# Softmax probabilities turned in two row halves of the matmul array

## The reference

```python
qkv = einsum('bte,fe->btf', layernorm(x), Wqkv)        # 8 heads of 64; q, k, v
q, k = q + pe, k + pe                                   # position table added
scores = einsum('bhtd,bhsd->bhts', q, k) / sqrt(64)     # causal mask
probs = softmax(scores, axis=-1)
attn = einsum('bhts,bhsd->bhtd', probs, v)
x = x + layernorm(attn_joined @ Wo.T)
x = x + layernorm(tanh(layernorm(x) @ W1 @ W2 @ W3 + bias))
```

## Time and profile before

| | |
|---|---|
| median of 3 runs | 561.28 us |
| the profiled execution | 561.25 us, span 559.4 us |
| PE busy | 537.3 us, 96% |
| PEld busy | 455.6 us, 81% |
| DVE busy | 469.5 us, 84% |
| ACT busy | 409.4 us, 73% |
| POOL busy | 398.9 us, 71% |

### The profile page before, as it was taken

The page is one execution under the profiler, slowest core; times in us unless marked ns, Lnnn a source line. Parts: engine busy times, 40 slices in busy tenths (PEclk is TensorE's granted clock), DMA queues, the critical chain, the costliest instruction groups (busy, mean ns, idle before and its releaser), DMA issues.

```text
span 559.4 us, 16795 instructions
## 1 busy us (share of the span) xinstructions
PE 537.3 (96%) x4595; PEld 455.6 (81%) x4595; DVE 469.5 (84%) x2063; ACT 409.4 (73%) x1507; POOL 398.9 (71%) x650
## 2 busy tenths in 40 slices
PE   7799999999999999999999999999999999999971
PEld 4588888888888888888888888888888888888850
DVE  4987898888889888888888888988888888888843
ACT  2777877778778777777877877777787787777740
POOL 3535777877777787777787777778777777776653
PEclk9999999999999999999999999999999999999985
DMA  5000011100000100000100010011000011100000
GB/s 160 29 2 21 11 30 30 30 19 28 20 18 28 28 28 19 28 17 21 28 28 25 22 28 9 28 28 28 19 28 24 14 28 28 28 9 21 21 9 19
DMA packets 27963, 14.53 MB, mean 26 GB/s; under 512 B 1700, under 2 KB 27431, under 8 KB 27943
## 3 DMA queue, kind: packets, MB, share of 16 engines
q1 hardware_dynamic: 27510, 13.51, 8.5%
q10 hardware_dynamic: 432, 0.79, 0.4%
HBM read 10.09 MB, written 4.19 MB: 26 GB/s over the span
## 4 chain that ended last, share of the span: by engine, by line
PE 92%; DVE 3%; ACT 2%; issue 1%; DMA 1%; POOL 1%; POOLq 0%; DVEq 0%; ACTq 0%
PE scores L879 18%; PE turned_and_heads L933 17%; PE misc_bank L994 11%; PE qk_bank L894 6%; PE qk_bank L896 5%; PE qk_bank L895 5%; PE turned_probs L910 5%; PE turned_probs L911 5%; PE turned_and_heads L919 5%; PE misc_bank L865 4%; PE misc_bank L977 3%; PE misc_bank L867 3%; PE misc_bank L866 3%; PE misc_bank L939 2%; PE misc_bank L975 1%
## 5 line engine op out<-in xcount | busy, mean ns | idle before, releaser
L263 ACT ACTIVATE probs<-scores,neg_max 128x256 f32<-128x256 f32 (+1 forms) x512 | 208.6, 425 | 43.4 <-DVE neg_max L631 43.3
L631 DVE CUSTOM_DVE_ANT_0 scores<-scores,mask 128x256 f32<-128x256 f32 (+1 forms) x512 | 166.2, 386 | 11.4 <-PE scores L879 11.4
L641 DVE TENSOR_TENSOR qk<-qk_bank,pe 128x512 f32<-128x512 f32 x128 | 87.4, 683 | 32.9 <-PE qk_bank L896 25.1
L421 POOL TENSOR_TENSOR probs<-probs,inv_sum 128x512 f32<-128x512 f32 x126 | 101.3, 823 | 12.6 <-DVE inv_sum L647 12.6
L879 PE MATMUL scores<-qk 64*128 64x256 f32 (+1 forms) x1024 | 106.6, 342 | 1.6 <-DVE qk L641 1.0
L263 ACT ACTIVATION_READ_ACCUMULATOR probs<-scores,neg_max 128x1 f32 x512 | 107.5, 210 | 0.0
L879 PEld LDWEIGHTS scores<-qk 64*128 64x128 f32 x1024 | 87.9, 186 | 18.7 <-issue 11.2
L933 PE MATMUL turned_and_heads<-pt,vals 128*64 128x256 f32 (+1 forms) x1024 | 98.5, 335 | 1.4 <-ACT pt L283 1.4
L933 PEld LDWEIGHTS turned_and_heads<-pt,vals 128*64 128x64 f32 x1024 | 64.6, 137 | 27.7 <-issue 2.0
L894 PE MATMUL qk_bank<-xt_hi,w_hi 128*128 128x256 f32 x256 | 80.5, 314 | 2.0 <-DVE qk L641 1.2
L281 ACT COPY pt<-turned_probs 128x512 f32<-128x512 f32 x128 | 76.4, 597 | 7.3 <-PE turned_probs L911 3.7
(11 more groups left out here) (91 smaller groups left out, 1013.8 us busy)
## 6 DMA issues: line engine op xcount, KB each, us to landing
x_in<-in_x SPq DMA_DIRECT2D x32, 128.0 KB, 2.2
x_res<-in_x SPq DMA_DIRECT2D x32, 128.0 KB, 2.1
out_x<-x SPq DMA_DIRECT2D x32, 128.0 KB, 1.8
w_raw<-in_w_qkv_t ACTq DMA_DIRECT2D x3, 256.0 KB, 3.8
pe<-pe_table SPq DMA_DIRECT2D x1, 256.0 KB, 5.2
wo<-in_w_o_t SPq DMA_DIRECT2D x1, 256.0 KB, 3.8
mask<-causal_mask SPq DMA_DIRECT2D x1, 128.0 KB, 5.3
w_sb<-in_w SPq DMA_DIRECT2D x2, 64.0 KB, 3.3
```

The costliest lines, as they stand in the source:

```text
L263: ins = nc.scalar.activation(probs[k][j][:, h, lo:hi], s_bank[j][:, h, lo:hi], ACT.Exp, bias=neg_max[k][j][:, i:i + 1], scale=-1.0, accum_ ...
L421: ins = nc.gpsimd.tensor_tensor(some, some, inv, ALU.mult)
L631: ins = nc.vector.tensor_tensor_reduce(some, some, mask[:, t * P:2 * P], -1.0, HIGHEST, ALU.add, ALU.min, neg_max[k][j][:, i:i + 1])
L641: nc.vector.tensor_tensor(qk[j][:, :], qk_bank[:, :], pe[:, :], ALU.add).then_inc(qk_kept, 1)
```

## The change

Each block of 128 x 128 is now turned as two blocks of 64 x 128 (rows 0 to 63 and rows 64 to 127), with a 64 x 64 piece of the identity as the moving operand. The two halves lie in the two row halves of the array and write into two different PSUM banks, so a turn is 12 instructions. The six blocks of a pair take columns 0 to 383 of both banks. `heads_bank` is now the second of these two banks. ACT's two copies each read from both banks and put the halves side by side. One semaphore, `turned`, replaces `turned0` and `turned1`. All of PE's waits for a turn stand ahead of its first instruction, followed by an increment of a semaphore that nobody waits for (`turn_begun`). turn_y stands ahead of turn (k=1, j=1) in place of behind it.

```diff
-        turn_bank = ps("turned_probs", [P, 2, T])
-        heads_bank = ps("turned_and_heads", [P, 512])
+        turned_banks = ps("turned_and_heads", [P, 2, 512])
+        heads_bank = turned_banks[:, 1, :]
...
                 wait(act, heads_made, units(b, k))
-                act.wait_ge(turned0, pairs(b, k, j + 1))
-                nc.scalar.copy(pt0[j][:, :, :], turn_bank[:, :, :]).then_inc(pt0_kept, 1)
-                act.wait_ge(turned1, pairs(b, k, j + 1))
-                nc.scalar.copy(pt1[j][:, :, :], heads_bank[:, 0:2 * P].rearrange("p (h t) -> p h t", h=2)
-                               ).then_inc(pt1_kept, 1)
+                act.wait_ge(turned, pairs(b, k, j + 1))
+                nc.scalar.copy(pt0[j][:, :, :].rearrange("p h (n f c) -> p (h n) f c", n=2, f=2),
+                               turned_banks[:, :, 0:T].rearrange("p f (n c) -> p n f c", c=D)).then_inc(pt0_kept, 1)
+                nc.scalar.copy(pt1[j][:, :, :].rearrange("p h (f c) -> p h f c", f=2),
+                               turned_banks[:, :, T:T + P].rearrange("p f (n c) -> p n f c", c=D)).then_inc(pt1_kept, 1)
...
                 wait(pe_eng, pt0_kept, pairs(b, k, j))
-                for h in range(2):
-                    nc.tensor.transpose(turn_bank[:, h, P:T], some[:, h, 0:P], ident[:, :])
-                    ins = nc.tensor.transpose(turn_bank[:, h, 0:P], some[:, h, T:SC], ident[:, :])
-                ins.then_inc(turned0, 1)
+                wait(pe_eng, pt1_kept, pairs(b, k, j))
                 if j == 0:
-
                     wait(pe_eng, heads_kept[(k + 1) % 2], b.times(1, k))
-                else:
-                    pe_eng.wait_ge(pt1_kept, pairs(b, k, 1))
-                for h in range(2):
-                    ins = nc.tensor.transpose(heads_bank[:, h * P:(h + 1) * P], some[:, h, P:T], ident[:, :])
-                ins.then_inc(turned1, 1)
+
+                pe_eng.sem_inc(turn_begun)
+
+                blocks = [(h, lo) for h in range(2) for lo in (T, 0)] + [(h, P) for h in range(2)]
+                for n, (h, lo) in enumerate(blocks):
+                    for f in range(2):
+                        r = slice(f * D, (f + 1) * D)
+                        ins = nc.tensor.transpose(turned_banks[:, f, n * D:(n + 1) * D], some[r, h, lo:lo + P], ident[r, r])
+                ins.then_inc(turned, 1)
...
                     turn_x(b.plus(1))
+                    turn_y(b.plus(-2))
                     turn_probs(b.plus(-1), 1, 1)
-                    turn_y(b.plus(-2))
                     make_scores(b, 1)
```

More of the change, by code:

```diff
@@ L145, in build_block @@
         scaled = [sem(f"scaled{j}") for j in range(2)]
-        turned0, turned1, pt0_kept, pt1_kept = sem("turned0"), sem("turned1"), sem("pt0_kept"), sem("pt1_kept")
+        turned, pt0_kept, pt1_kept = sem("turned"), sem("pt0_kept"), sem("pt1_kept")
+        turn_begun = sem("turn_begun")
         heads_made, heads_kept = sem("heads_made"), [sem(f"heads_kept{k}") for k in range(2)]
@@ L256, in exps @@
                     return
-                wait(act, turned1, pairs(b, k, j - 3))
+                wait(act, turned, pairs(b, k, j - 3))
                 act.wait_ge(max_found, pairs(b, k, j + 1))
```

## The result

The changed kernel takes 558.31 us (median of 14 runs, 557.06 to 560.59) against 561.13 us for the kernel before on the same chip (14 runs, 560.46 to 562.21): a ratio of 0.9952, 95% interval 0.994 to 0.9964. It is faster, by 2.8 us. The forecast was 9.3 us. Its profiled execution took 557.18 us with a span of 555.3 us, 4.1 us less than the span before. It is one of the five quickest of the 14 (557.06 to 557.23 us), so the two traces show more of a gain than the medians do.

What follows compares the result with a forecast made beforehand. PE, busy 96% of the span, was taken as the bound. One turn with its scores saves 0.30 us a batch, the others zero: 561.25 - 31 x 0.30 (9.3) = 552.0 us, range 545 to 564.

Steps and rivals of the forecast that it cites:

- The distance between pairs: In each new turn, pairs of half-row transposes start 0.06 us apart, with bounds 0.055 and 0.11 us.
- The change of shape: Between full-array and row-half work on PE: 0.09 us for emptying, plus up to 0.10 for an unhidden weight load.
- The lone turn (1, 0): Turn (k=1, j=0), changing shape twice: make_qk +0.03 us at most; ACT's copy late by 0.02 to 0.07 us.
- No gain behind the turn (1, 1): Scores after turn (k=1, j=1): PE could gain 0.28 us but waits that long for the DVE and ACT loop.
- No gain behind the turn (0, 0): After turn (k=0, j=0): the next weight load waits for ACT's copy of attn until 285.69, so zero gain.
- DVE in time at the scores behind the turn (0, 1): At these scores DVE is ready at 288.71, the scores come at 288.78, so DVE just lets the gain through.
- The term 31 x 0.30: Turn (k=0, j=1) with its scores saves 0.30 us per batch, 31 times between batches: 9.3 us.
- the end of the kernel: Behind the loop, ACT gets its first table after six pairs instead of four transposes: 0.3 us either way.
- the waits that moved: Earlier `heads_kept` and `pt1_kept` waits ahead of all twelve transposes: free, late bookkeeping taken at zero, bounds 0 and 0.12 us.
- Copies dearer, or the sequencer late: Rival, chance 0.13: +0.16 to +0.28 us a batch on the binding loop, 557 to 561 us.
- Both pairs gain: Rival, chance 0.12: more slack in the DVE and ACT loop lets 0.28 us come too, 18 us, 543 us.
- The distance does not shrink: Rival, chance 0.19: pairs stay 0.11 us apart, turns only add changes of shape, +0.37 x 32 = 11.8, 573 us.

Runs made afterwards that it cites:

- the cut in before: Kernel before with two 128-column ScalarE exponentials left out of each loop batch (output wrong there): period 16.30 us against 16.46; 556.39 us, one run.
- the filled pair: Kernels before and after, each with matmuls on zeros in PE's idle gaps behind the loop: 559.97 and 555.11 us, tails 42.10 and 43.20 us.
- the unfilled tails: Last batch's value projections to the end, profiled kernels without matmuls on zeros: full turns 42.35 to 43.42 us, halves 44.86 to 46.57.
- the two kernels with the cut: Kernels before and after, each with two 128-column ScalarE exponentials left out of each loop batch: periods 16.30 and 15.80 us, 0.50 apart.

## Why the prediction was wrong

**What held.** The distance between pairs: 0.06 us, as taken from the second weight load in the earlier trace rows, and so the bound on the whole change was read rightly. The change of shape, 0.09 us on either side. The lone turn (1, 0) at +0.03 us on PE. No gain behind the turn (1, 1), with PE waiting for ACT instead. The copies at their old price. No gain behind the turn (0, 0). DVE in time at the scores behind the turn (0, 1): its wait for them fell from 11.4 to 0.9 us in all. The Trainium skill states in "TensorEngine Tiling (Array Packing)", section Key Properties, that a change of the tiling mode drains the array; the 0.09 us ahead of the first pair of halves (283.54 + 0.12 to 283.75) agrees.

**The term 31 x 0.30 was mis-sized by 2.1 us.** It measured 29 x 0.25 = 7.2 us at the last batch's value projections. The turn with its scores saved 0.28, by the kernel that has it alone: the score load behind the last pair cost 0.07 us (284.11 to 284.18) in place of the 0.11 taken, but the second score pair came 0.27 us behind the first (284.18 to 284.45). It had been 0.32 before (287.96 to 288.28), and the prediction had struck off 0.10, down to 0.22. Another 0.02 is the lone turns, whose lateness at ACT (0.02 to 0.07) the prediction had worked out, found to be within ACT's slack, and left out of the sum: with the turn (0, 1) alone the period is 16.17, with all four 16.20, with the two lone ones 0.04 above before's. And the offset between the two kernels grows only from batch 3 on: at batch 2 they stand at 39.03 and 39.00 us. PE does not set the time there alone: it was busy for 14.36 of the 17.70 us from 4.3 to 22.0 in after. The prediction also took PE for the bound of the kernel before; by the cut in before, a chain through ACT was longer by 0.16 us, and the gain came in only because the turn (0, 1) lies on that chain too.

**The step that failed is the end of the kernel**, "0.3 us either way". It measured +3.04 us in the profiled runs, and 4.0 us by the medians where that form was put into before's tail, 3.5 where it was taken out of after's. The step looked at one effect only, that ACT gets its first table after six pairs in place of four transposes. It did not carry over its own paragraph on the waits that moved. That paragraph found `heads_kept` free because DVE's copy ends 0.73 us before it is needed, in the loop; it said that without this cover the cost would be the lateness itself. In the tail, nothing stands between make_heads and the next turn, the cover is gone, and the lateness is about 0.9 us at one turn. The trace of before gives the warning at two turns of the last batch, (0, 1) and (1, 1), and at make_heads between them:

```profile
532.67 0.30 PE L910 MATMUL turned_probs<-ident,probs 128*128 128x128 f32 x1 [0.98 <-ACT pt L281]
...
534.35 2.65 PE L933 MATMUL turned_and_heads<-pt,vals 128*64 128x256 f32 x16 [0.83 <-ACT pt L283]
...
539.13 0.33 PE L910 MATMUL turned_probs<-ident,probs 128*128 128x128 f32 x1 [0.83 <-DVE probs L728]
```

Two of these waits are for ACT's copies, the third is for the division on DVE. Where PE waits for a copy, a copy that starts later moves PE by as much.

Then the lost time had an echo. The array was idle for longer, and its clock was granted in half for 10.2 us in place of 3.4 between the turns of the last batch. The prediction read PEclk as "in full nearly throughout" in the earlier trace rows and did not ask what the 8 and the 5 in the last slices would become. By the filled pair this is nearly twice the size of the wait itself, 1.9 against 1.1 us; by the unfilled tails the two are about equal.

**The rivals.** "Copies dearer, or the sequencer late" gave 557 to 561 us and held the measured time, but for a reason that did not occur: the copies cost what they did, and the loop gained. "Both pairs gain" did not come in time, but the two kernels with the cut indicate that PE itself gained about 0.5 us a batch. It was the chain over DVE and ACT that held the rest back, as the forecast said. "The distance does not shrink" is refuted by the 0.06 us. It had leant on a rule of the Trainium skill, "TensorE: Matmul & The Clock Gate", section LDWEIGHTS, by which a load costs its columns over 1.2 in ns: 0.107 us here. The trace disagrees for these loads, and the measurement decides.

**What stays open.** Why the clock comes back so late after the halves and not after the full turns: the fillers show that PE's idle time in the tail is what brings it down, not which of the gaps does. Tails of one form do not always have the same stretch: with full turns three of five profiled ones had none, and with halves one of four had 3.4 us in place of 10.2. And no run takes the earlier waits or the bare increment away alone; in the loop no more than the 0.02 and 0.04 us put down to the lone turns is left for them.

## What to carry to other kernels

- Work a moved wait out at every place where the code runs, the fill and the tail too. A cover read in the steady loop (here 0.73 us) says nothing of a place where the work around it is missing.
- Merging two banks that are released at different times couples their releases. Half of the work could start early here because its bank was nobody else's.
- Change the one place that stands on the path. Halves at one turn out of four gave the whole gain of the loop (0.28 us a batch) and none of the loss at the end: 553.5 us, and 552.7 with the gaps of the tail filled, against 558.3 and 561.1.

## What the chip showed that was not expected

- Idle gaps in the tail cost twice: once as time, once by the clock that follows. With 37 matmuls on zeros in the gaps, the tails of the two kernels are 1.10 us apart in place of 3.04, and the granted clock over the tail of after goes from 0.78 to 0.97. By the medians the filler is worth 3.2 us where the clock had been low for 10.2 us; where it had been low for 3.4, 1.4 us, which is not clear of noise.
- Two row halves of a transpose, written to two banks, follow each other at 0.06 us a pair, weight load of 128 columns included, half the distance of a full one. For a lone turn this is eaten up by the two changes of shape: 0.84 us in place of 0.81.
- ScalarE's copy out of two banks, in runs of 64 elements, costs the same as one out of a single bank: 0.60 us for 512 elements and 0.40 for 256 (means of 128 each).
